# Start of the second feed-forward pass moved into the last attention unit, with no barrier between the two

## The reference

```python
x = x + 0.5 * ffn(_layernorm(x), W_syn, b_syn, W_out, b_out, gamma, beta)
x = x + attn(_layernorm(x), ...)
x = x + 0.5 * ffn(_layernorm(x), W_syn, b_syn, W_out, b_out, gamma, beta)
```

## Time and profile before

| | us |
|---|---|
| median of three runs (1247.32 to 1249.38) | 1247.36 |
| the profiled execution | 1247.17 |
| its span, first to last instruction | 1245.4 |
| TensorE busy, share of the span | 1089.0, 87% |
| VectorE busy | 893.8, 72% |
| ScalarE busy | 804.1, 65% |
| GpSimd busy | 367.0, 29% |

### The profile page before, as it was taken

The page is one execution under the profiler, slowest core; times in us unless marked ns, Lnnn a source line. Parts: engine busy times, 40 slices in busy tenths (PEclk is TensorE's granted clock), DMA queues, the critical chain, the costliest instruction groups (busy, mean ns, idle before and its releaser), DMA issues.

```text
span 1245.4 us, 18065 instructions
## 1 busy us (share of the span) xinstructions
PE 1089.0 (87%) x5941; PEld 492.7 (40%) x5990; DVE 893.8 (72%) x2229; ACT 804.1 (65%) x1193; POOL 367.0 (29%) x400
## 2 busy tenths in 40 slices
PE   0788999998869889999999799999799899998886
PEld 0334455544434333232344223332244345554443
DVE  4788888889943887885335787883133888898893
ACT  5489888888524446566614355667337888888862
POOL 2101234444560143101220451002100124434456
PEclk9999999999978889999999899999899999999998
DMA  9200000000020221210000221110000000000000
GB/s 367 90 1 1 1 1 2 1 1 1 1 56 1 51 69 44 52 36 1 1 21 9 72 57 35 44 36 2 1 1 1 1 1 18 19 18 15 21 18 35
DMA packets 22287, 37.45 MB, mean 30 GB/s; under 512 B 5398, under 2 KB 7833, under 8 KB 21532
## 3 DMA queue, kind: packets, MB, share of 16 engines
q1 hardware_dynamic: 21404, 34.54, 8.8%
q0 software_dynamic: 768, 1.57, 0.5%
HBM read 19.17 MB, written 4.21 MB: 19 GB/s over the span
## 4 chain that ended last, share of the span: by engine, by line
PE 58%; DVE 23%; issue 8%; POOL 3%; SPq 3%; ACT 2%; DMA 1%; DVEq 1%; another core or an unknown queue 1%; POOLq 0%; ACTq 0%
PE zP L502 12%; PE oP L554 9%; PE xP L664 5%; PE oP L664 5%; PE zP L592 5%; PE zP L648 4%; PE hP L629 3%; DVE arena L1248 3%; DVE m L1256 3%; PE hP L524 2%; PE zP L689 2%; PE hP L689 2%; DVE scored L1446 2%; PE zP L629 2%; DVE arena L1468 1%
## 5 line engine op out<-in xcount | busy, mean ns | idle before, releaser
L802 ACT ACTIVATE arena<-arena,X 128x2048 int8<-128x2048 f32 x154 | 307.9, 2005 | 4.7 <-DVE X L1228 4.7
L857 ACT ACTIVATE arena<-zP,asc 128x512 f32<-128x512 f32 (+3 forms) x384 | 200.6, 582 | 109.2 <-PE zP L652 78.7
L502 PE MATMUL zP<-T,arena 128*128 128x512 f16 x1024 | 248.8, 387 | 0.7
L554 PE MATMUL oP<-T,arena 128*128 128x512 f16 x832 | 199.7, 384 | 1.4 <-DVE arena L1343 1.4
L502 PEld LDWEIGHTS zP<-T,arena 128*128 128x128 f16 x1024 | 102.1, 100 | 123.0 <-issue 11.4
L758 ACT ACTIVATE arena<-zP,sc 128x512 f32<-128x512 f32 x128 | 87.5, 688 | 87.0 <-PE zP L507 54.4
L554 PEld LDWEIGHTS oP<-T,arena 128*128 128x128 f16 x832 | 82.0, 99 | 79.8 <-issue 5.5
L648 PE MATMUL zP<-arena 98*128 98x512 f16 (+3 forms) x384 | 110.5, 334 | 2.8 <-DMA arena<-arena 1.9
L1468 DVE RECIPROCAL arena<-arena 128x128 f32<-128x128 f32 x64 | 57.1, 926 | 61.7 <-ACT arena L870 61.7
L629 PE MATMUL hP<-arena 96*128 96x512 f16 (+3 forms) x256 | 84.0, 351 | 15.6 <-DVE mx L1446 12.1
L973 POOL TENSOR_SCALAR ln<-ln 128x1 f32<-128x1 f32 x32 | 38.5, 1204 | 198.3 <-DVE ln L1172 198.2
(11 more groups left out here) (195 smaller groups left out, 1846.3 us busy)
## 6 DMA issues: line engine op xcount, KB each, us to landing
arena<-arena SPq DMA_DIRECT2D x168, 64.0 KB, 2.0
arena<-in_w_synT SPq DMA_DIRECT2D x4, 1024.0 KB, 8.3
arena<-in_w_outT SPq DMA_DIRECT2D x4, 1024.0 KB, 14.9
out_dram<-x_sb SPq DMA_DIRECT2D x16, 256.0 KB, 2.0
x_sb<-in_x SPq DMA_DIRECT2D x3, 1024.0 KB, 14.0
arena<-in_w_o SPq DMA_DIRECT2D x2, 1024.0 KB, 5.1
arena<-arena POOLq DMA_DIRECT2D x24, 64.0 KB, 1.9
arena<-in_b_syn SPq DMA_DIRECT2D x1, 1024.0 KB, 12.1
```

Of the source, the lines that this page charges most:

```text
L502: pe.matmul(zP[:, c * CW:(c + 1) * CW], part[:, g % 2, k, :], T1[:, k, c * CW:(c + 1) * CW], start=(n == 0 and k == 0), stop=False)
L554: mm = pe.matmul(o, part[:, k, :], T2[:, k, :], start=(c == 0 and n == 0 and k == 0), stop=False)
L802: act.activation(junk[:, counted[0] % 2, :], Z[:, g % ZR, :], ACT.Sign, bias=X[:, 2, k:k + 1], accum_out=S[:, k:k + 1]).then_inc(sm["cnt"], 1)
L857: act.activation(PT[:, m // 4 % 2, h, q0:512], colP[m % 3][:, q0:512], ACT.Exp, scale=asc[:, g, 10:11]).then_inc(sm["exp_done"], 1)
```

## The change

The second pass no longer starts behind a barrier. In the second core, VectorE, GpSimd, TensorE and ScalarE each do their part for tile 0 of the second pass (and VectorE and GpSimd the statistics and normalization of tile 1) at a named place of the last two units. The turn of tile 0 goes to the free bank `hP[:, 0, :]` instead of `xP`. TensorE then begins the first product of tile 0 behind the last attention matmul; the output projections stand behind the products, one in slot 1, two in slots 2, 3 and 4, and one in slot 5 (before: two in slot -1 and one in each of the slots 0 to 5). Waits on single results take the place of the barrier.

```diff
         def out_tiles(f, s):
-            return () if f == 0 else (0, 1) if s == -1 else (s + 2,) if 0 <= s < BT - 2 else ()
+            return {1: (0,), 2: (1, 2), 3: (3, 4), 4: (5, 6), 5: (7,)}.get(s, ()) if f else ()
+
+        def x_bank(f, i):
+            return hP[:, 0, :] if (f, i) == (1, 0) else xP[:, :]
...
# TensorE, x_turn
+                if (f, i) == (1, 0):
+                    pe.wait_ge(sm["row_max"], 2 * TOTAL["row"])
+                    pe.wait_ge(sm["m_rows"], 2 * TOTAL["turn"])
+                elif (f, i) == (1, 1):
+                    pe.wait_ge(sm["sum_out"], 2 * TOTAL["norm"])
# TensorE, mm1
+                    if (f, i) == (1, 0):
+                        pe.wait_ge(sm["exp_done"], 2 * TOTAL["col"])
# TensorE, core
+                        if b == 1 and e[1:] == (GROUPS - 1, 1, 4, 0):
+                            x_turn(1, 0)
# all five engines, behind the core of b
-                        barrier(pe, 2 + b)
+                        if b == 0:
+                            barrier(pe, 2 + b)
# ScalarE, x_hi and core
+                if (f, i) == (1, 0):
+                    act.wait_ge(sm["mix_done"], TOTAL["mix"] + TOTAL["mix"] * (GROUPS - 1) // GROUPS)
+                        if b == 1 and e[1:] == (GROUPS - 1, 1, 6, 0):
+                            x_hi(1, 0)
# GpSimd, core, ahead of the product m
+                    if b == 1 and m >= TOTAL["norm"] - 2:
+                        rstd1(1, m - TOTAL["norm"] + 2)
# VectorE, normal
+                if f == 1 and i < 3:
+                    dve.wait_ge(sm["attn_set"], 2 * TOTAL["norm"] - 2 + i)
+                elif f == 1 and i < 6:
+                    dve.wait_ge(sm["mix_done"], 2 * TOTAL["mix"])
# VectorE, core
+                    elif kind == "norm" and b == 1 and m >= 2 * TOTAL["norm"] - 3:
+                        u = m - 2 * TOTAL["norm"] + 3
+                        if u < 2:
+                            stats1(1, u)
+                        if u:
+                            normal(1, u - 1)
+                        if u == 2:
+                            x_lo(1, 0)
```

More of the change, by code:

```diff
@@ L463, in _ @@
                 max_rows(3, 1)
-                barrier(eng, 2 + b)
+                if b == 0:
+                    barrier(eng, 2 + b)
             ov = out.rearrange("(t p) d -> p t d", p=P)
@@ L485, in x_turn @@
                     pe.wait_ge(sm["ok_read"], f * NT + i - S_SEL)
+                if (f, i) == (1, 0):
[3 more added lines that the diff above has]
+                    pe.wait_ge(sm["sum_out"], 2 * TOTAL["norm"])
                 for k in range(KD):
-                    mm = pe.transpose(xP[:, k * P:(k + 1) * P], xn[:, g % XR, k * P:(k + 1) * P], identf[:, :])
+                    mm = pe.transpose(x_bank(f, i)[:, k * P:(k + 1) * P], xn[:, g % XR, k * P:(k + 1) * P], identf[:, :])
                 mm.then_inc(sm["xT_ps"], 1)
@@ L700, in _ @@
                         do(h_turn, f, s, S_OUT, c)
-                        if c == 0 and (f, s) != (0, 0):
+                        if c == 0 and s:
                             do(x_turn, f, s, 0)
@@ L731, in x_hi @@
                     act.wait_ge(sm["z_ps"], 4 * (g - 2) + 4)
-                act.activation(xThi[:, g % 2, :, :].rearrange("p k t -> p (k t)"), xP[:, :], ACT.Copy,
+                if (f, i) == (1, 0):
+                    act.wait_ge(sm["mix_done"], TOTAL["mix"] + TOTAL["mix"] * (GROUPS - 1) // GROUPS)
+                act.activation(xThi[:, g % 2, :, :].rearrange("p k t -> p (k t)"), x_bank(f, i), ACT.Copy,
                                scale=XSCALE).then_inc(sm["xT_hi"], 1)
@@ L905, in _ @@
                     do(h_hi, f, s, S_OUT, 0)
-                    if (f, s) != (0, 0):
+                    if s:
                         do(x_hi, f, s, 0)
@@ L924, in _ @@
                             take_rows(1)
-                        barrier(act, 2 + b)
+                        if b == 0:
+                            barrier(act, 2 + b)
         def counts_before(f, s):
@@ L1047, in _ @@
                     do(rstd2, f, s, S_FIN)
-                    do(rstd1, f, s, -1)
+                    if f == 0 or s > 0:
+                        do(rstd1, f, s, -1)
                     if f == 0 and s == 0:
@@ L1062, in _ @@
                             rstd_rows(1, range(2, BT))
-                        barrier(pool, 2 + b)
+                        if b == 0:
+                            barrier(pool, 2 + b)
         @block.vector
@@ L1166, in stats1 @@
                     dve.wait_ge(sm[f"x_in{i // 4}" if i else "x_first"], 16)
-                elif i >= BT:
+                else:
                     dve.wait_ge(sm["x_att"], i + 1)
+                if (f, i) == (1, 1):
+                    dve.wait_ge(sm["stats1"], g)
                 link(dve.bn_stats(st6[:, 0:6], x_sb[:, i, :]))
@@ L1186, in x_lo @@
                 dve.wait_ge(sm["xT_hi"], g + 1)
-                dve.scalar_tensor_tensor(xTlo[:, g % 2, :, :].rearrange("p k t -> p (k t)"), xP[:, :], XSCALE,
+                dve.scalar_tensor_tensor(xTlo[:, g % 2, :, :].rearrange("p k t -> p (k t)"), x_bank(f, i), XSCALE,
                                          xThi[:, g % 2, :, :].rearrange("p k t -> p (k t)"), ALU.mult,
@@ L1498, in _ @@
                         update(f, s)
-                    early = s <= S_OUT and (f, s) != (0, 0)
+                    early = s <= S_OUT and s
                     if early:
@@ L1508, in _ @@
                     do(h_lo, f, s, S_OUT, 0)
-                    if not early and (f, s) != (0, 0):
+                    if not early and s:
                         do(x_lo, f, s, 0)
@@ L1515, in _ @@
                     residual(f, s)
-                    if (f, s) != (0, -1):
+                    if s > -1 and (f, s) != (1, 0):
                         do(stats1, f, s, -1)
@@ L1535, in _ @@
                         core(b)
-                        barrier(dve, 2 + b)
+                        if b == 0:
+                            barrier(dve, 2 + b)
 def kernel(**inputs):
```

## The result

The changed kernel takes 1238.56 us (median of five runs, 1234.73 to 1241.13), the kernel before 1247.94 in the same rounds (1247.32 to 1250.76). The ratio is 0.9921, with an interval of 0.9904 to 0.9938: 0.8% faster. The profiled execution took 1239.19 us, 7.98 less than that of before.

A forecast was written before the change was run, and what follows sets the result against it. TensorE's 8.76 us hole at the seam, ended by GpSimd's drain, and 1.62 us of low clock behind it were the loss; removing both (10.38) from 1247.17 gave 1236.79, forecast 1236.8 us, range 1235.0 to 1239.5.

The forecast's parts named there:

- The hole: Between second attention core and second pass: TensorE's 8.76 us idle goes if tile 0's split input is ready.
- The low clock: TensorE from 893.96 to 906.31: three projections and one turn take 10.73 us at full clock, 1.62 less.
- The turn: Turn of tile 0 moves into the last unit: TensorE pays 0.44 us there and saves 0.44 after it.
- Moved projections at no cost: Projections of tiles 0 to 2 move behind products in slots 2 to 4: 10.29 us moved, not saved.
- The list of margins: Seam steps' ends against when TensorE wants them: 10.9 us to spare for normalized tile 0, 0.8 at tile 1's turn, the tightest.
- The sum: Fifth slot ends at 954.13 instead of 964.51, 10.38 us earlier (8.76 + 1.62), giving 1236.8 us.
- The slower rival's price: TensorE stops mid last unit at the turn, normalized tile 0 missing: 1249.7 us and more; chance 0.03.
- Its condition: For over 0.2% slower, normalized tile 0 would have to be 23.8 us later than the 863.0 found.
- The clock further on: Near 989.07, TensorE's slow stretch after 2.66 us idle costs 1.6 us; the sum keeps it.
- the rival: Slow stretches fall otherwise after the shift: 1235.2 or 1238.4 us; chance 0.13.
- its 1238.4: Time in us if another idle of that kind is followed by a slow stretch too.
- The rival's lower value: 1235.2 us, if after the shift the idle near 989.07 isn't followed by a slow stretch.

The follow-up runs named there:

- the filled hole: Kernel before, barrier kept, with 34 unused matmuls ahead of TensorE's drain in the hole: 1245.55 us beside 1247.64, ratio 0.9985.

## Why the prediction was right, and where it was off

- *The hole* (8.76): shown. With the barrier back it is there again to the hundredth, and the gain is gone.
- *The low clock* (1.62): shown, 1.51 by the filled hole. It isn't a constant of the kernel: behind the same hole, with a product there instead of projections, it was 3.0 in one profile.
- *The turn* (0.44 paid, 0.44 saved): it took 875.29 - 874.79 = 0.50. The first product came 886.47 - 866.23 = 20.24 us behind the first mark; the sum had 885.64 - 865.38 = 20.26.
- *Moved projections at no cost*: shown; first or behind the product, 88.83 and 88.75.
- *The list of margins* held within 0.2 us: tile 0 normalized at 863.7 for a turn at 874.79 (11.1 to spare, 10.9 forecast); its split at 882.6 for 886.47 (3.9, 3.8); the bank of the sums read until 887.7 for a turn at 888.42 (0.7, 0.8); tile 2 normalized at 895.7 for 900.07 (4.4, 4.3).
- *The sum*: 88.75 between the marks was forecast (954.13 - 865.38), and 88.75 was measured, in three profiles of the changed kernel. It isn't errors that cancel: up to the first product the sum is 0.02 too long, and from there (885.64 to 954.13 = 68.49, measured 954.98 - 886.47 = 68.51) 0.02 too short.
- *The slower rival's price*: a stop of TensorE in the middle of a unit does arrive one for one, with the low clock on top. Its condition was far from met.
- *The clock further on*: this is the term that was mis-sized, both in the sum and as a rival. The sum kept the slow stretch of slot 8 "as it is"; in the profiled execution it was longer and the part behind the seam took 1.5 us more. That this is close to the 1.6 of the rival is in part luck: its 1238.4 was worked out for another idle that is followed by a slow stretch too, and what came was a longer stretch behind the same idle. The rival's lower value took all of 1.6 us off for a slow stretch that goes; with the idle filled, only 41.46 - 40.95 = 0.5 comes off the stretch of before, so 1236.3 and not 1235.2. The profile that the sum started from also had the cheapest slow stretch of the nine (41.46 against 41.59 to 43.31), which makes a sum that keeps it come out low. The Trainium skill, "TensorE: Matmul & The Clock Gate", Part 1, says that the watch over TensorE's activity isn't aligned with the program; the traces agree: same program, same idle of 2.66 us, a bank of 3.62 in one execution and 2.65 in another.
- *What the text left out* is that the part ahead of the change varies too. The first mark moves over 5.7 us between executions. That the one pair of profiles lay 0.85 apart is chance. The medians of the changed kernel came out at 1238.56, 1238.60 and 1236.54, so 1236.8 is at the low end of what is measured. The 2.06 between the three runs shown was too little to judge the spread by: single runs of the kernel before went from 1244.72 to 1253.15, though its medians in the four sets of rounds (1246.89 to 1248.26) lie within 1.4. Other than for the 0.85, which stretches ahead of the first mark make up its 5.7 us stays open.

## What to carry to other kernels

Here the all-engine barrier cost the busiest engine the longest tail of the others (8.76 us) plus what the clock did behind the idle (1.5 to 3.0), and the hole could be read to a hundredth before the change. Look at what really needs that tail and prepare the first tile inside idle time of the others; whether the product or the projections came first then made no difference. Forecast such a change between two marks that all engines share, not in total time: here the sum was right to a hundredth between the marks while the total moved by microseconds. Before you build on a slow stretch of one profile, look at several: it was there in nine of nine and cost anything from 0.5 to 2.4 us. And unused work in a short idle of TensorE took those off in slot 8, gave 0.7 back when it was longer than the idle, and earned nothing in slot 17, where TensorE doesn't carry the path.

## What the runs showed of the hardware that was not expected

- Executions differ ahead of any change: the first mark came at 862.27 to 868.01 us with TensorE and ScalarE doing the same work up to it. Behind the third mark, 239.4 to 239.5 us long, nothing differed, though the clock falls there too (granted 0.83 from 1140 to 1150 in the changed kernel).
- An idle of 2.66 us in slot 8, behind two others of 1.3 to 1.5 us, was followed by slow stretches of different length, in nine of nine profiles: four transposes at 0.66 to 1.12 us, the next bank at 2.52 to 3.62; with the idle filled, 0.66 and 1.89 in all three.
- The same hole of 8.76 us cost 1.5 us of clock with projections behind it and 3.0 with the first product, in one profile each.
